# One batch's token sum: from sixteen products of ones on TensorE to seven additions on GpSimd, and a small product moved behind the last slots

## The reference, cut to what matters

```python
logits   = einsum('bmd,dnp->bmnp', x, phi)        # x: 2 x 2048 x 256, phi: 256 x 64 x 32
dispatch = softmax(logits, axis=0)                # over the batch, which has two elements
combine  = softmax(logits over (n p), axis=-1)
slots    = einsum('bmd,bmnp->bnpd', x, dispatch)
y        = einsum('bnpd,nde->bnpe', slots, W) + b
out      = einsum('bnpd,bmnp->bmd', y, combine)
```

## Time and profile before

| | |
|---|---|
| time, median of 3 runs | 636.65 us (636.16 to 637.34) |
| the profiled execution's own time | 636.62 us |
| its span, first to last instruction | 634.7 us |
| TensorE busy | 625.1 us, 98% |
| VectorE busy | 453.8 us, 71% |
| ScalarE busy | 360.2 us, 57% |
| GpSimd busy | 219.1 us, 35% |

### The profile page before, as it was taken

One profiled execution on the slowest core, in us unless ns is written; L12 is line 12 of the kernel. 1 busy time (PEld: TensorE's weight loads), 2 busy tenths in 40 slices (PEclk: granted clock), 3 DMA queues, 4 the chain that ended last, 5 costly groups with the idle time before them and its releaser, 6 DMA issues.

```text
span 634.7 us, 15295 instructions
## 1 busy us (share of the span) xinstructions
PE 625.1 (98%) x5327; PEld 393.7 (62%) x5327; DVE 453.8 (71%) x898; ACT 360.2 (57%) x695; POOL 219.1 (35%) x377
## 2 busy tenths in 40 slices
PE   8999999999999999999999999999999999999996
PEld 8898645444444444444444456777777777777775
DVE  5987999935443644436243499999888888888886
ACT  5666868642333232323544466777766666666664
POOL 5355766620000000000000001555555555555554
PEclk9999999999999999999999999999999999999999
DMA  8920032226766666665456522222222222222201
GB/s 273 400 78 1 12 72 50 61 61 162 207 194 198 193 171 173 191 186 159 127 153 180 174 77 67 93 91 91 91 91 91 91 91 91 91 91 91 91 17 34
DMA packets 78772, 77.07 MB, mean 121 GB/s; under 512 B 6417, under 2 KB 75282, under 8 KB 76434
## 3 DMA queue, kind: packets, MB, share of 16 engines
q1 hardware_dynamic: 76256, 74.34, 38.5%
q10 hardware_dynamic: 2482, 2.29, 1.0%
HBM read 51.71 MB, written 23.07 MB: 118 GB/s over the span
## 4 chain that ended last, share of the span: by engine, by line
PE 86%; DVE 8%; issue 2%; POOL 1%; ACT 1%; DMA 1%; SPq 0%; POOLq 0%; ACTq 0%; DVEq 0%
PE psL L1587 26%; PE psM L1574 12%; PE psL L1704 11%; PE psM L1722 7%; PE psM L1726 7%; PE psM L1723 7%; PE psM L1604 4%; PE psL L1474 2%; PE psM L1532 2%; PE psL L1790 1%; DMA xres<-in_x 1%; PE psL L1532 1%; PE psM L1481 1%; DVE r_y L1120 1%; DVE small L1307 1%
## 5 line engine op out<-in xcount | busy, mean ns | idle before, releaser
L1587 PE MATMUL psL<-r,r_xn 128*128 128x512 f16 x768 | 176.3, 379 | 1.4 <-DVE r L1129 1.3
L1587 PEld LDWEIGHTS psL<-r,r_xn 128*128 128x128 f16 x768 | 73.4, 98 | 91.8 <-issue 6.7
L774 ACT ACTIVATE r<-psM,small 128x512 f32<-128x512 f32 x64 | 43.8, 684 | 100.6 <-PE psM L1574 100.6
L1574 PE MATMUL psM<-phs,xx 128*128 128x512 f16 (+1 forms) x384 | 93.2, 379 | 0.3 <-DVE xx L1166 0.3
L591 POOL MEMSET r_xn<- 128x8 f16 x2 | 0.3, 139 | 229.1 <-PE psL L1587 229.1
L1127 DVE TENSOR_SCALAR r<-r 128x512 f16<-128x512 f32 x64 | 28.1, 439 | 68.2 <-ACT r L774 68.1
L1704 PE MATMUL psL<-phs,r 128*32 128x512 f16 x1344 | 75.1, 379 | 0.0
L507 POOL TENSOR_TENSOR small<-small,epst 128x2 f32<-128x2 f32 (+3 forms) x77 | 60.2, 784 | 19.7 <-DVE small L1153 11.8
L1574 PEld LDWEIGHTS psM<-phs,xx 128*128 128x128 f16 x384 | 37.4, 98 | 45.1 <-issue 1.1
L886 ACT ACTIVATE r<-psL,small 128x512 f32<-128x512 f32 x60 | 41.9, 777 | 37.6 <-DVE small L1334 37.4
L1704 PEld LDWEIGHTS psL<-phs,r 128*32 128x32 f16 x1344 | 34.6, 97 | 36.5 <-issue 3.0
(11 more groups left out here) (205 smaller groups left out, 1255.1 us busy)
## 6 DMA issues: line engine op xcount, KB each, us to landing
r<-in_ffn_w SPq DMA_DIRECT2D x23, 1024.0 KB, 5.8
logit_difference<-r SPq DMA_DIRECT2D x256, 64.0 KB, 1.9
xx<-logit_difference SPq DMA_DIRECT2D x16, 1024.0 KB, 4.8
out<-r SPq DMA_DIRECT2D x32, 128.0 KB, 1.7
xres<-in_x SPq DMA_DIRECT2D x6, 512.0 KB, 10.3
r<-in_phi SPq DMA_DIRECT2D x1, 2048.0 KB, 15.9
expert_bias<-r ACTq DMA_DIRECT2D x1, 2048.0 KB, 21.2
r<-expert_bias SPq DMA_DIRECT2D x16, 128.0 KB, 5.4
```

Of the source, the lines that this page charges most:

```text
L774: nc.scalar.activation(tF[:, j % 2, :], bk[j % 2][:, :], ACT.Sigmoid, scale=kap[:, 0:1]).then_inc(t_ready, 1)
L1574: ins = mm(bk[j % 2][:, :].rearrange("p (q m) -> p q m", q=EP), xxT[:, 1, j, hx, k, :], phw[:, hp, k, :, bass.ds(nb, 1), :].rearrange("p q ...
L1587: ins = mm(psL[:, i * 512:(i + 1) * 512], x3n[:, b, j, hx, k * P:(k + 1) * P], thl[:, j % 2, hs, :], start=(j == 0 and hx + hs == 0), stop ...
```

## The change

The block of ones, `token_sums` and `token_sums_copy` go. GpSimd adds the fp32 tokens of batch 1 in seven additions `token_sum(p)` of 128x512, pair by pair, each waiting for the one before it. They stand between and behind its last `x3_lo`. `x3_terms(1, 7)` moves ahead of `x3_lo(0, 7)`. `half_sums` now waits for the seven additions and moves from ahead of `slots_first(15)` to behind it. Its constant column loses the factor 1/32, since the ones product had made 32 equal rows of each sum. ScalarE's `half_sums_copy` keeps its place.

```diff
-        ones16 = sb("ones16", [P, Q], F16)
-            own.add(nc.gpsimd.memset(ones16[:, :], 1.0))
-            own.add(nc.gpsimd.memset(q_mean, 1.0 / (Q * X_SCALE)))
+            own.add(nc.gpsimd.memset(x_mean, 1.0 / X_SCALE))
...
+            def token_sum(p):
+                pool.wait_ge(x3_ready, X_AT[1, p] + 1)
+                if p >= 2:
+                    pool.wait_ge(xs_added, p - 1)
+                nc.gpsimd.tensor_tensor(xsum.rearrange("p (t c) -> p t c", t=2),
+                     xsum.rearrange("p (t c) -> p t c", t=2) if p > 1 else xy[:, 1, 0:2, :],
+                     xy[:, 1, 2 * p:2 * p + 2, :], ALU.add).then_inc(xs_added, 1)
...
-            y_terms(1, 7); x3_terms(0, 7); x3_lo(1, 6); x3_lo(0, 7); x3_terms(1, 7); x3_lo(1, 7)
+            y_terms(1, 7); x3_terms(0, 7); x3_lo(1, 6); token_sum(1); token_sum(2); x3_terms(1, 7)
+            x3_lo(0, 7); token_sum(3); token_sum(4); x3_lo(1, 7); token_sum(5); token_sum(6); token_sum(7)
...
-            def token_sums_copy():
-                act.wait_ge(xs_done, 1)
-                copy(xsum, bk[3][:, :]).then_inc(xs_copied, 1)
...
-            x3_float(1, 7); x3_hi(1, 7); tanh(0, 13); xd_hi(7); d_copy(0, 13); token_sums_copy()
+            x3_float(1, 7); x3_hi(1, 7); tanh(0, 13); xd_hi(7); d_copy(0, 13)
             tanh(0, 14); d_copy(0, 14); tanh(0, 15); d_copy(0, 15); half_sums_copy()
...
-            def token_sums():
-                pe.wait_ge(y_added, B * NJ)
-                pe.wait_ge(xdl_ready, NJ // 2)
-                pe.wait_ge(x3l_ready, B * NJ // 2)
-                for r in range(NJ // GJ):
-                    for g in range(GJ):
-                        ins = mm(bk[3][g * Q:(g + 1) * Q, :], ones16[:, :],
-                                 x3n[:, 1, r * GJ + g].rearrange("p h c -> p (h c)"), start=(r == 0), stop=(r == NJ // GJ - 1))
-                ins.then_inc(xs_done, 1)
             def half_sums():
-                pe.wait_ge(xs_copied, 1)
+                pe.wait_ge(xs_added, NJ // 2 - 1)
...
-            token_sums(); d_first(14); slots_first(13); d_first(15); slots_first(14); d_tile(1, 0)
-            half_sums(); slots_first(15); d_tile(1, 1)
+            d_first(14); slots_first(13); d_first(15); slots_first(14); d_tile(1, 0)
+            slots_first(15); half_sums(); d_tile(1, 1)
```

More of the change, by code:

```diff
@@ L220, in build @@
         wm, pbm = sm.take(K), sm.take(2)
-        q_mean, xtotal = sm.take(1), sm.take(K * B)
+        x_mean, xtotal = sm.take(1), sm.take(K * B)
         def per_token():
@@ L282, in build @@
             sem("xd_turned"), sem("ident16_ready"), sem("x1_turned"), sem("x1_copied"))
-        xs_done, xs_copied, xtotal_done, xtotal_ready = (
-            sem("xs_done"), sem("xs_copied"), sem("xtotal_done"), sem("xtotal_ready"))
+        xs_added, xtotal_done, xtotal_ready = sem("xs_added"), sem("xtotal_done"), sem("xtotal_ready")
         d_done, t_ready, d_copied, s_split, slots_used = (
@@ L1620, in slots_first @@
                 slots(0, j)
-            def token_sums():
-                pe.wait_ge(y_added, B * NJ)
-                pe.wait_ge(xdl_ready, NJ // 2)
-                pe.wait_ge(x3l_ready, B * NJ // 2)
-                for r in range(NJ // GJ):
-                    for g in range(GJ):
-                        ins = mm(bk[3][g * Q:(g + 1) * Q, :], ones16[:, :],
-                                 x3n[:, 1, r * GJ + g].rearrange("p h c -> p (h c)"), start=(r == 0), stop=(r == NJ // GJ - 1))
-                ins.then_inc(xs_done, 1)
             def half_sums():
-                pe.wait_ge(xs_copied, 1)
+                pe.wait_ge(xs_added, NJ // 2 - 1)
                 for k in range(K):
                     for h in range(2):
-                        ins = mm(bk[2][:, k:k + 1], xsum[:, h * C + k * P:h * C + (k + 1) * P], q_mean,
+                        ins = mm(bk[2][:, k:k + 1], xsum[:, h * C + k * P:h * C + (k + 1) * P], x_mean,
                                  start=(h == 0), stop=(h == 1))
```

## The result

The changed kernel takes 638.55 us (median of 11 runs, 637.91 to 639.21), the kernel before beside it 636.74 us (11 runs, 636.16 to 637.46): ratio 1.0027, 95% interval 1.0019 to 1.0034, or 1.8 us slower (1.2 to 2.2). The forecast was 1.65 us slower, 638.3. The profiled execution has a span of 636.1 us against 634.7. Among the executions timed for the experiments two were far slower than the rest, one of e2 (1679 us) and one of the kernel before (723 us); no ratio counts them, and they move their medians by at most 0.03 us.

What follows compares the result with a forecast made beforehand. TensorE, busy 98% of the span, was taken to bound the kernel. Removed products -1.07, wait for xd_lo(7) +0.97 and wait at slots(1, 0) +1.75 gave +1.65 us, 638.3; range 636.9 to 639.6 with rivals (a) and (c).

Steps and rivals of the forecast that it cites:

- The removed products: TensorE near 134 us: without the sixteen products d_first(14) could start at 133.88 instead of 134.95, a gain of 1.07 us.
- The waits for VectorE: Near 128 to 134 us: VectorE takes turns with GpSimd's additions, so xd_lo(7) ends at 134.7 instead of 133.53.
- the end of the turns: First place, d_first(14): depending on who gets each turn, between -0.6 and +0.3 us, taken as -0.1.
- the 0.97 us for the wait for `xd_lo(7)`: TensorE at d_first(14): the wait for xd_lo(7) takes the place of the removed products, +0.97 us.
- additions of 1.45 us or more: GpSimd's seven 128x512 additions: about 1.16 us each was forecast; 1.45 or more would show the prediction wrong.
- the 0.45 us that I worked out: TensorE at turn_xd(7): start at 131.3 instead of 130.85, 0.45 us lost, not added since the xd_lo(7) wait ends later.
- The moved products: Border of the blocks: half_sums_copy, ahead of tanh(1, 0) on ScalarE, comes later; TensorE waits 1.75 us at slots(1, 0).
- What passes through: Behind the border: later stages keep their lengths, so 1.7 us pass to the end; SyncE's later load costs 0 to +0.3.
- (a): Rival: port conflict costs the path nothing, gain of 1.07 stays, border costs 1.75; together +0.7, 637.3 us; chance 0.15.
- (b): Rival: the border costs nothing and the products' gain stays, -1.07, 635.6 us; with the port conflict 636.55; chance 0.12.
- (c): Rival: additions of 1.45 us, with both split parts and transposes each waiting for one; +2.65, 639.3 us; chance 0.12.
- (d): Rival: the sum isn't ready and half_sums waits; needs over 10 us more on GpSimd; no chance of its own given.

Runs made afterwards that it cites:

- e2: Kernel before without the sixteen products of ones and ScalarE's copy of their result, no token sum computed instead; 635.53 us, ratio 0.9983.
- e3: Changed kernel with half_sums back ahead of slots_first(15), the additions on GpSimd kept; 636.74 us, ratio 1.0003 to the kernel before.
- e5: Changed kernel with half_sums' result copied by VectorE just ahead of slots_out and additions 3 to 7 behind fold_weights; 635.58 us, ratio 0.9982 to the kernel before.
- e1: Kernel before with only half_sums moved behind slots_first(15), products of ones kept, no additions on GpSimd; 638.50 us, ratio 1.0031.
- e8: Changed kernel with half_sums back ahead of slots_first(15) and each addition replaced by a one-input multiplication by one; 635.09 us, ratio 0.9978 to the kernel before.

## Why the prediction was right, step by step

**The removed products.** 1.07 us forecast, 1.09 by the stretch of e2.

**The waits for VectorE.** The mechanism was right and each link came: the low part of `split(0, 12)`, `xd_diff(7)`, the transposes behind it, the low part of `split(0, 13)`, then `xd_lo(7)`. The size was low. The forecast for this place was -0.1 us, the runs show +0.35 (e3), a little beyond the +0.3 that I gave as the end of the turns, within the +0.9 of longer additions. The term of the sum that was mis-sized is the 0.97 us for the wait for `xd_lo(7)`: by e2 and e3 it is 1.44. The larger part of the miss is the length of an addition: 1.16 us taken from the earlier trace rows, against this (line L576 of the changed kernel: ns min/median/max, first and last start):

```profile
L576 POOL TENSOR_TENSOR r<-r,r_y x6: 1263/1450/1535, 123.7 to 135.2; 128x512 f32<-128x512 f32 x6
```

The shortest is 1.26, and the others carry their own waits for VectorE. (The row has six; `token_sum(1)` has another form and took 1.45.) The prediction named additions of 1.45 us or more as a sign of being wrong; the recorded median is just that, but it holds waits, and GpSimd's own time is 1.26. Three additions lie in the path (3, 4 and 5), so 0.1 on each makes 0.3 of the 0.45. Another 0.2 is a start that I set too early: `x3_lo(0, 7)` at 126.7, though in the kernel before the terms that it needs end only at 126.73 + 0.20 = 126.93.

```profile
126.73 0.20 POOL L565 TENSOR_TENSOR small<-small 128x2 f32<-128x2 f32 x1
```

In the changed trace it starts at 126.14, which is 126.88 on the time of before (0.74 us on, by `slots_first(11)`). So the high part of `split(0, 12)`, which I had let pass, met it and took 0.67 instead of 0.43 (in e5 too, where no addition is near), and addition 3 waited for that one. Together `xd_lo(7)` ended at 134.50 + 0.74 = 135.24 instead of 134.7; the wake-up of TensorE behind it was 0.06 instead of 0.15 to 0.2, which takes 0.1 off again.

**A wait sized by its position.** At the transposes TensorE lost more than the 0.45 us that I worked out: they start 4.76 us behind `slots_first(11)` in the changed kernel (130.99 - 126.23) and 3.88 before (130.85 of the earlier trace rows less 126.97), 0.88 us. As said there it isn't to be added: `xd_lo(7)` was later still.

**The moved products.** 1.75 us forecast, 1.71 by e1. The links were 0.27, 0.72, 0.46 and 0.61 from the end of the small products to the first bank (147.18, 147.45, 148.17, 148.63, 149.24), against 0.28, 0.72, 0.46 and 0.60. The bank and the wake-up took 0.80 (149.24 to 150.04), against 0.85 to 0.9. So the term of the border, 1.75 us, needs no correction.

**What passes through.** Nothing behind the stretch gave anything back or took anything, as the sum assumed (586.0 and 586.1 us): 2.06 us in the stretch and 1.8 in the medians (1.2 to 2.2 by the interval) agree. By the stretch the forecast of 1.65 was 0.4 us short; that the median came within 0.25 us of 638.3 is partly the luck of the scatter. SyncE's later load shows as one wait of 0.21 us of VectorE ahead of the maximum of `Wx`, with no wait of TensorE behind it:

```profile
153.23 2.29 DVE L1210 TENSOR_REDUCE small<-r 128x2048 f32 x1 [0.21 <-DMA r<-in_ffn_w]
```

**The rivals.** (a), that GpSimd's additions cost VectorE's path nothing, is excluded by e3, and (b), that the border costs nothing, by e1. (c), the longer additions, was half right: they are longer, by a tenth and not by a quarter. (d) didn't happen: the last addition ended at 131.91 + 4.53 = 136.44, on the time of before 137.2 against the forecast 136.5, and `half_sums` started 9.8 us later; the prediction had put this slack at over 10.

## What to carry to other kernels

Where an engine's program is a fixed order, the place of a consumer counts more than that of its producer: before moving a product later, look up what waits for it and what stands behind that wait, on every engine. Work moved to an idle GpSimd isn't free for VectorE: place it where VectorE's operations between SBUF tensors have slack, or cut it into shorter operations where it must stand in a tight stretch. A saving of 1.07 us was real and was had (e5), but only with both consumers put right.

## What the runs showed of the hardware

VectorE and GpSimd take turns, whole operations at a time, where VectorE's inputs lie in SBUF alone. VectorE's 128x512 operation with two SBUF inputs took up to 1.64 to 1.75 us instead of 0.69 beside GpSimd's 1.26 us additions, 1.10 to 1.21 beside ones of half the length, 0.99 beside one-input operations of 0.62 us, and the next operation begins 0.15 us before the recorded end of the other's. Its operation with a single SBUF input (the high part of a split) was held too, 1.20 us instead of 0.43. Its operation with one of two inputs in PSUM took 0.68 in all of them. The Trainium skill (SBUF — State Buffer, section Terms) calls the port pair that the two share exclusive, held for the whole instruction, with the loser fully blocked. These rows agree. The hand-over shortly ahead of the recorded end is read from the rows alone.

What I hadn't expected is how much less GpSimd's operation with one input takes: 128x512 in fp32 is 0.62 us as a multiplication by one (e8) and 1.26 as an addition of two inputs, twice as much. The two also differ in the kind of operation, so that the second input alone isn't shown to be the cause.
